# Pacing the gathers of expert results by a count of matrix products, and where the last graphs' sums stand

## The reference

```python
x = x + elu(feat @ W_1 + softmax(masked leaky_relu logits) @ feat @ W_2)      # per graph, feat = layernorm(x)
f = layernorm(x)
gate_logits = f @ gate_w + gate_b
topk_vals, topk_idx = jax.lax.top_k(gate_logits, K)                           # K = 2 of E = 16
topk_w = jax.nn.softmax(topk_vals, axis=-1)
h = jax.nn.relu(jnp.einsum('bsh,ehf->bsef', f, w1) + b1)                      # 128 -> 256
expert_out = jnp.einsum('bsef,efh->bseh', h, w2) + b2                         # 256 -> 128
y = f + sum over the two chosen experts of topk_w * expert_out
x = x + (y - mean(y)) / sqrt(var(y) + EPS) * gamma + beta
```

## Time and profile before

| | |
|---|---|
| timed runs | 551.95, 555.43, 561.11 us (median 555.43) |
| profiled execution | 558.59 us |
| its span in the trace | 557.0 us |
| TensorE busy | 445.4 us, 80% |
| VectorE busy | 410.2 us, 74% |
| ScalarE busy | 317.9 us, 57% |
| GpSimd busy | 308.9 us, 55% |
| gathers (line 652) | 128, 123.4 us busy, from 327.9 to 544.0 us |

### The profile page before, as it was taken

How to read it: one execution, slowest core, us unless ns; L and a number is a source line. 1 busy time by engine, 2 the same in 40 slices (tenths; PEclk the granted TensorE clock), 3 DMA queues, 4 the chain that set the end, 5 groups by cost and what they waited for, 6 DMA issues and landing times.

```text
span 557.0 us, 11259 instructions
## 1 busy us (share of the span) xinstructions
PE 445.4 (80%) x3049; PEld 378.2 (68%) x3071; DVE 410.2 (74%) x1807; ACT 317.9 (57%) x860; POOL 308.9 (55%) x336
## 2 busy tenths in 40 slices
PE   7899999999888998887886887988869789796100
PEld 5577767776666776666786877978859789695000
DVE  5557988888888889778665676497758678676845
ACT  3888877787788887774564334544444545343000
POOL 3202477767667777556455535664554555644770
PEclk9999999999999999997899799798998799979555
DMA  7646748535644342821033345465545556534331
GB/s 233 227 128 223 214 179 221 202 129 205 203 163 160 81 179 101 243 86 40 24 101 82 109 113 140 102 156 156 147 127 145 142 152 166 139 87 128 98 82 47
DMA packets 86402, 78.83 MB, mean 142 GB/s; under 512 B 13971, under 2 KB 71747, under 8 KB 85062
## 3 DMA queue, kind: packets, MB, share of 16 engines
q1 hardware_dynamic: 77574, 60.99, 36.9%
q0 software_dynamic: 8192, 16.86, 10.7%
q10 hardware_dynamic: 576, 0.26, 0.2%
HBM read 44.44 MB, written 33.65 MB: 140 GB/s over the span
## 4 chain that ended last, share of the span: by engine, by line
PE 35%; DVE 33%; issue 14%; another core or an unknown queue 7%; ACT 6%; POOL 3%; DVEq 1%; ACTq 1%; DMA 0%; POOLq 0%
PE bank L1052 11%; PE bank L1034 11%; DVE bn L1114 3%; DVE prob L1130 3%; DVE no_edge L1108 3%; PE bank L1021 2%; DVE row_out L1172 2%; POOL yy L652 2%; PE bank L923 2%; PE bank L884 2%; DVE x_sb L1155 2%; DVE mv L1119 2%; DVE z L1143 2%; ACT hidT L801 2%
## 5 line engine op out<-in xcount | busy, mean ns | idle before, releaser
L596 POOL DMA_INDIRECT expert_bins<-row_out,slots x128 | 135.8, 1061 | 79.7 <-DVE slots L1341 36.9
L652 POOL DMA_INDIRECT yy<-expert_results,slots x128 | 123.4, 964 | 99.8 <-ACT hidT L801 48.5
L801 ACT ACTIVATE hidT<-bank,b_cols 128x128 f32<-128x128 f32 x316 | 87.3, 384 | 110.4 <-remote 62.2
L1034 PE MATMUL bank<-xgT,w_cur 128*128 128x128 f32 x632 | 88.8, 289 | 20.8 <-issue 18.0
L1052 PE MATMUL bank<-w_sb,hidT 128*128 x632 | 91.1, 300 | 9.9 <-issue 6.2
L1034 PEld LDWEIGHTS bank<-xgT,w_cur 128*128 128x128 f32 x632 | 81.6, 204 | 24.1 <-issue 22.0
L1404 DVE SCALAR_TENSOR_TENSOR y<-bank,xg 128x128 f32<-128x128 f32 x158 | 46.9, 342 | 65.9 <-remote 53.5
L1052 PEld LDWEIGHTS bank<-w_sb,hidT 128*128 128x128 f32 x632 | 83.7, 211 | 11.5 <-issue 11.2
L902 PEld LDWEIGHTS bank<-vh,probT 128*128 128x128 f32 x512 | 64.1, 194 | 16.5 <-issue 13.9
L902 PE MATMUL bank<-vh,probT 128*128 128x128 f32 x512 | 66.4, 278 | 2.1 <-ACT probT L684 2.1
L894 PE MATMUL bank<-featT,qT 128*128 128x512 f32 x128 | 65.3, 592 | 1.3
(11 more groups left out here) (155 smaller groups left out, 710.0 us busy)
## 6 DMA issues: line engine op xcount, KB each, us to landing
adj_sb<-in_adj_dram SPq DMA_DIRECT2D x16, 1024.0 KB
expert_bins<-xg SPq DMA_DIRECT2D x10, 1032.0 KB, 8.4
expert_results<-y SPq DMA_DIRECT2D x78, 128.0 KB
xg<-expert_bins SPq DMA_DIRECT2D x38, 258.0 KB
x_sb<-in_x_dram SPq DMA_DIRECT2D x16, 256.0 KB
out_dram<-x_sb SPq DMA_DIRECT2D x15, 256.0 KB
expert_bins<-row_out,slots POOLq DMA_INDIRECT x128
yy<-expert_results,slots POOLq DMA_INDIRECT x128
```

The source lines that it names most:

```text
L596: nc.gpsimd.indirect_dma_start(bins[u], bass.IndirectOffsetOnAxis(ap=slots[:, g, i, j:j + 1], axis=0), row_out[:, r, j, i, :], None).then_ ...
L652: nc.gpsimd.indirect_dma_start(yy[:, b, i, j * D:(j + 1) * D], None, results[0:rows, :], bass.IndirectOffsetOnAxis(ap=slots[:, g, i, j:j + 1],
L801: r = nc.scalar.activation(hidT[:, t % NB, c * P:(c + 1) * P], hidden_of(t, c), ACT.Relu, bias=b1_cols[:, bass.ds(e * FC + c, 1)])
L1034: m1 = mm(hidden_of(t, c), w1_cur[:, t % WS, c * P:(c + 1) * P], xgT[:, t % NB, :], start=True, stop=True)
```

## The change

Three edits. The pace of the gathers counts matrix products in place of relu pairs: TensorE raises the new semaphore `s_pace` with the first matmul (c = 0) of each tile in either layer, 2 x 158 = 316 raises, and gather n waits for 60 + 12n/5 of them (capped at 316, so gathers 107 to 127 wait for the last). STATS has graphs 0 to 10 in place of 0 to 13: of those that were dropped, only graph 11's statistics (behind tile 156) and centring (behind tile 157) stood inside the loop; all else of graphs 11 to 14 stood behind it already. And the last graph is summed as three tiles and one in place of two and two.

```diff
-    LAST_PARTS = ((0, 2), (2, 4))
-    FIRST_PAIRS = 16
+    LAST_PARTS = ((0, 3), (3, 4))
+    FIRST_PRODUCTS = 60
...
+        s_pace = sem("expert_product_begun")
...
-        STATS = {g: 46 + 10 * g for g in range(G - 2)}
+        STATS = {g: 46 + 10 * g for g in range(G - 5)}
...
-        def pairs_for_gather(g, n):
-
-            return min(FIRST_PAIRS + (g * TPG * K + n) * 3 // 5, NT // 2)
+        def products_for_gather(g, n):
+
+            return min(FIRST_PRODUCTS + (g * TPG * K + n) * 12 // 5, 2 * NT)
...
-                        pool.wait_ge(s_hr, pairs_for_gather(g, i * K + j))
+                        pool.wait_ge(s_pace, products_for_gather(g, i * K + j))
...
                             m1 = mm(hidden_of(t, c), w1_cur[:, t % WS, c * P:(c + 1) * P], xgT[:, t % NB, :], start=True,
                                     stop=True)
+                            if c == 0:
+                                m1.then_inc(s_pace, 1)
...
                         m2 = mm(out_psum(t), hidT[:, t % NB, c * P:(c + 1) * P],
                                 w2_sb[:, bass.ds((e * FC + c) * D, D)], start=False,
                                 stop=(t == batch(b)[-1] and c == FC - 1))
+                        if c == 0:
+                            m2.then_inc(s_pace, 1)
```

## The result

The changed kernel takes 530.92 us (median of 4 runs, 529.70 to 531.35) against 553.69 for the kernel before beside it (548.75 to 561.11): ratio 0.9614, 95% interval 0.9539 to 0.9689. Ratios compare fast runs alone (runs over 1.5% above the fastest of their kernel are left out), while medians are of all runs, so that a ratio can differ a little from the quotient of two medians.

A forecast was written before the change was run, and what follows sets the result against it. Stops ending about when a run of indirect DMAs has drained cost the expert loop 49 us. Only the tail's -1.3 counted: 558.59 became 557.3 profiled, or 554 us for timed runs 3.16 lower; 8-in-10 range 538 to 563.

The forecast's parts named there:

- term 2: Expert loop: when the new count lets gathers go; taken as 0, with bounds of -21 and +21 us.
- shorter runs: Rival, expert loop: later, single permits shorten gather runs at stops; 543 us at half the bound, 533 whole; chance 0.31.
- Term 1: TensorE: 316 matmuls get a semaphore raise and no instruction is added; 0, at most 2 us.
- Term 3: Start of the last gathers: gather 107 at about 516.4 for 517.68; -1.3 us, with 0 and +2 as other cases.
- Term 4: Graph 11 behind the loop: tile 157's result comes 2.1 us earlier, hidden by some 14 us; 0.
- Term 5: Last graph's sums on VectorE: three tiles take 4.1 us, one 2.3; 0, bounds -0.3 and +0.8.
- Longer runs: Rival, expert loop: after a stop TensorE's count leads the relus, so gather runs join; +11, 565 us; chance 0.14.
- Nothing in the loop moves: Rival, expert loop: GpSimd's own step and stored results bind; 555.4, or 554 with the tail; within the likeliest case, 0.55.
- The rule on instruction fetches: Stops as late instruction fetches would follow the number of instructions; pacing would change nothing in the loop.
- the signs I had named: Among them: GpSimd's gather waits name TensorE; ScalarE's and VectorE's unknown waits stay near 61 and 40 us.

The follow-up runs named there:

- m1: The kernel before with every gather let go two pairs of relus later (FIRST_PAIRS 18 for 16), chip C: 553.5 us, 1.002 of the kernel before.
- k3: The changed kernel with the product count a gather waits for rounded to the nearest multiple of 8, chip B: 536.9 us, 0.966 of the kernel before.
- k2: The changed kernel with the old pace by relu pairs and no raises on TensorE, chip B: 550.4 us, 0.990 of the kernel before.
- k1: The changed kernel with STATS and LAST_PARTS as before, so only the new pace of gathers, chip B: 529.6 us, 0.953 of the kernel before.
- h1: The changed kernel itself, run again on chip B: 530.5 us, 0.957 of the kernel before.
- f1: The changed kernel with STATS and LAST_PARTS as before, so only the new pace of gathers, chip A: 470.9 us, 0.999 of the kernel before.
- h2: The changed kernel without any pace for gathers and no raises on TensorE, chip B: 596.1 us, 1.078 of the kernel before.
- k4: The changed kernel without any pace, but with at most two gathers under way, chip B: 555.7 us, 1.002 of the kernel before.

## Why the prediction was wrong

**The step that failed is term 2**: "Both signs have an example (steadier permits, and a count that leads ScalarE), so I take 0 and keep -21 and +21 as bounds." The term came to its lower bound: 31 batches at 5.19 for 5.86 us are -20.7. The mechanism was that of the rival "shorter runs", whose whole size I had put at 533 and whose half I took as its centre; 530.92 came. The bound's working (one gather fewer in each of 17 runs) was wrong in both factors and right in sum by luck: rows went from five to seven down to three, a row of seven costs a stop of 5.9 us where three cost 1.3, and about half of the 20.7 us is not a shorter stop at all but TensorE's busy time, 11.2 us, with the lower clock behind the long stops in it. No term of mine had the clock.

What should have moved me stood in my own text. The old count is raised by ScalarE, which has relus to catch up when a stop ends: that is the wait of 2.81 us until 478.55 and the row up to 486.04 in the earlier trace rows. I called the permits' number per batch equal and concluded a direct worth of 0; it is how many of them come together behind a stop that counts. That ScalarE's catching up makes the row is argued from these rows. Against too simple a picture speaks that TensorE's raises come in bunches too: at 443.0 in the changed kernel five of them arrive within 0.3 us, which is two gathers. What the runs show is that lateness doesn't explain the gain (m1) and fineness only a part of it (k3), so that the counter's engine remains; why it matters is open.

**The other terms.** Term 1, the raises, 0: shown on chip A, where the new count gives 0.999 and 4.32 us a batch. Term 3, -1.3: not there. Gather 107 started on GpSimd's own step, at 492.24, 3.8 us behind TensorE's last product (488.42), and the last gather stands 35.5 or 35.6 us behind batch 39 in both. I had named this case (the term is 0 if no stop falls there). Term 4, 0: it held as far as it can be seen; k2, with terms 4 and 5 alone, is at 0.990, and its profile is 4.5 us shorter behind batch 39 than the 49.4 of before. But k1, without them, has the same 45 us there (45.2 against 44.9), so the tail varies with where a stop falls, and I can't give those edits a worth of their own. Term 5, 0: the part of three tiles took from 517.69 to 523.57, 5.9 us and not 4.1, because VectorE waits between its own short steps (1.09 us before the variance, for its own count); the part of one took 2.4, as worked out (2.3). Its price didn't show in k1 against h1, 529.55 and 530.50.

**The rivals.** "Longer runs" fell: GpSimd's waits became shorter but the rows did too. "Nothing in the loop moves" is true of chip A alone (4.32 and 4.33 us a batch). **The rule on instruction fetches** (the Trainium skill, "Runtime: NRT & Kernel Launch", "Instruction fetch mechanics") is out as the cause here: the kernels differ by at most 32 instructions among 11259 to 11291 and take from 524 to 596 us, and of the 13 waits of ScalarE over 2 us for an unknown releaser between batches 0 and 39 of the changed kernel 8 have no packet of either instruction queue inside (q8, which I had looked at, and q14, which I had not). That fetches are mostly hidden, as the page says, agrees with these traces: f1 has the same 27 packets on q8, one of them 1.89 us long, and no such stop.

**Of the signs I had named**, GpSimd's waits do name TensorE, and ScalarE's and VectorE's unknown waits fell to 44.9 and 28.8, just under the 45 and 30 well below which I had set "shorter runs". My chances leaned on one argument, that I could not sign the effect; with the stops' end tied to a row's end in 17 cases, the trace had already pointed to the length of a row as the price.

## What to carry to other kernels

Where other engines stop until a row of indirect DMAs has drained, break up the rows: let two or three go at a time, by a count that the engine whose work you want to keep moving raises as it goes. Here a count of TensorE's products did better than one of ScalarE's relus, whether it came earlier or later. Look at the length of rows, not at the mean rate, and look at the granted clock and at TensorE's busy time beside its idle time: a long stop can cost twice. And before anything is tuned on such stops, time the kernel on a second chip.

## What the chips showed that I had not expected

**Chips differ by 15%.** The kernel before took 471.26 us on chip A and 551.7 to 558.7 on B, C and D, where its single runs lie between 549.3 and 565.7 (470.1 to 475.1 on A). Between the profiles of f1 and of the kernel before, the loop accounts for 48 us of the difference (134 for 182), the stage from batch 0 to batch 8 for 17 (46.5 for 63.4), all before batch 0 for 16 (246.6 for 262.6), and what is behind batch 39 for 8. The change is worth nothing on A and 4 to 5% on B and D. The median first-layer matmul in the loop takes 275 ns in f1, in the changed kernel and in the kernel before, but TensorE's busy time for the same loop is 133.1, 142.5 and 153.7 us: it is the stops, the instructions let out singly in them, and the lower clock behind the long ones. Why one chip has none stays open.

**What is late in a stop.** The unknown releaser is mostly TensorE itself. By the semaphore updates in the trace, each of the 25 waits over 2 us of ScalarE and VectorE that the profile calls "remote" between batch 0 and 515 us of the kernel before ends on a count that TensorE alone raises, as do all 23 of the changed kernel; the raise comes 1.8 to 6.7 us (changed: 1.5 to 6.3) behind the end that the trace gives for its matmul. In f1, on chip A, none of TensorE's counts of the two layers comes over 1 us late from batch 8 to batch 39. The kernel before, in the stop of the earlier trace rows, and at the end:

```profile
484.29 0.27 PE L1021 MATMUL bank<-ident,xg 128*128 128x128 f32 x1 [0.51 <-issue]
485.75 0.27 PE L1021 MATMUL bank<-ident,xg 128*128 128x128 f32 x1 [1.19 <-issue]
487.19 0.33 PE L1021 MATMUL bank<-ident,xg 128*128 128x128 f32 x1 [1.17 <-issue]
488.60 0.37 PE L1021 MATMUL bank<-ident,xg 128*128 128x128 f32 x1 [1.08 <-issue]
...
540.71 0.17 DVE L1425 TENSOR_SCALAR final_var<-final_mv 128x4 f32<-128x4 f32 x1 [2.44 <-remote]
```

TensorE lets out one transpose in 1.4 us, and the counts of both layers, whose matmuls the trace ends at 481.99 and 483.77, arrive at 488.72 and 488.90; VectorE and ScalarE start at once (488.74, 488.93). They stand because they wait for TensorE. At 540.71 TensorE has long finished, and VectorE waits for a count of its own, which arrives at 540.68, 2.4 us behind the instruction that raises it (538.27). So it isn't TensorE alone, but what the cases have in common is a raise that comes late. In h2 VectorE's adds, statistics and copies ran at their usual lengths in the midst of the stop (506.9 to 511.8); GpSimd keeps its step throughout.

**What holds them is open too.** The ends of matmuls are modelled in the trace, so it can't tell a late matmul from a late raise. The Trainium skill's page "GPSIMD Engine Reference" (section "Specifications") names an interface to SBUF that GpSimd shares with VectorE; it doesn't cover TensorE's single matmuls, and the same program on chip A has no such stop. Whether it is the writing of descriptors or the transfers themselves was not separated: k4 bounds both. Nor is it known whether the recording of the trace has a part in the stops: it holds 34 of the 40 raises of the second layer's count in the kernel before, and all 40 in f1.
